# Turning the graph operator, the attention context and the gated input by DMA instead of on TensorE, in a four-layer graph kernel

## What is computed

```
x = LN(x + L0(x, adj))   # hypergraph convolution, relu, LN, convolution, + x
x = LN(x + L1(x, adj))   # softmax over nodes of q . (adj k), times v
x = LN(x + L2(x, adj))   # 8-head attention, scores times 2 adj
x = LN(x + L3(x, adj))   # gate from the row sums of adj, scores times adj

# L0's operator, used twice; H = (adj != 0)
P = Dn * (H @ (Be * H^T))         # Dn = 1 / (H w), Be = 1 / column counts
# L2
ctx = softmax(q k^T * scale * 2 adj) v ;  L2 = ctx Wo^T + bo
# L3
xg = x * sigmoid(deg * wd + bd) ;  QK = sigmoid(xg Wqk^T + bqk)
L3 = relu(normalised(QK QK^T * adj) xg Wl^T + bl + xg Wr^T)
```

## Time and profile before

| | |
|---|---|
| median of three runs | 952.0 us |
| the profiled execution | 954.0 us, span 952.2 us |
| PE, DVE, ACT, POOL busy, share of the span | 91%, 80%, 77%, 71% |
| mean granted PE clock | 0.974 |
| DMA packets, of these under 512 B | 194573, 112866 |

### The profile page before, as it was taken

The page is one execution under the profiler, slowest core; times in us unless marked ns, Lnnn a source line. Parts: engine busy times, 40 slices in busy tenths (PEclk is TensorE's granted clock), DMA queues, the critical chain, the costliest instruction groups (busy, mean ns, idle before and its releaser), DMA issues.

```text
span 952.2 us, 34347 instructions
## 1 busy us (share of the span) xinstructions
PE 871.1 (91%) x12124; PEld 755.5 (79%) x12124; DVE 764.7 (80%) x2292; ACT 730.8 (77%) x1740; POOL 678.1 (71%) x1005
## 2 busy tenths in 40 slices
PE   3668999999999999999999999999999999998754
PEld 2557778888888888888888888888888888886642
DVE  4757787888888888888888888888888888887651
ACT  2466578888888888888888888888888888877551
POOL 2566677778777778877877777887787777774440
PEclk9799899999999999999999999999999999999985
DMA  7003453443444344444444444444434443444420
GB/s 210 20 15 97 109 114 73 103 114 102 111 124 122 100 115 110 113 104 119 104 109 124 121 100 116 108 113 104 120 100 113 124 121 100 116 99 125 119 46 22
DMA packets 194573, 99.46 MB, mean 104 GB/s; under 512 B 112866, under 2 KB 194276, under 8 KB 194532
## 3 DMA queue, kind: packets, MB, share of 16 engines
q1 hardware_dynamic: 194532, 98.93, 40.5%
HBM read 48.28 MB, written 25.17 MB: 77 GB/s over the span
## 4 chain that ended last, share of the span: by engine, by line
PE 30%; SPq 22%; DVE 14%; DMA 14%; issue 10%; ACT 6%; POOL 3%; DVEq 0%; ACTq 0%; POOLq 0%
PE bank L537 7%; PE bank L538 7%; PE bank L539 7%; DMA Ks<-k_by_head 6%; SPq L426 6%; DMA k_by_head<-kst 6%; SPq L402 5%; SPq L374 3%; SPq L387 3%; DVE Ehl L1288 2%; DVE stG L1126 2%; PE bank L562 2%; PE bank L738 2%; DVE preG L1347 2%; PE bank L815 1%
## 5 line engine op out<-in xcount | busy, mean ns | idle before, releaser
L1375 POOL TENSOR_TENSOR rFl<-r,rFh 128x512 f16<-128x512 f32 x64 | 73.1, 1162 | 25.5 <-ACT rFh L826 25.5
L537 PE MATMUL bank<-z1h,W 128*128 128x256 f16 x256 | 71.7, 280 | 4.7 <-DVE z1l L1025 4.6
L538 PE MATMUL bank<-z1l,W 128*128 128x256 f16 x256 | 71.7, 280 | 0.0
L539 PE MATMUL bank<-z1h,W 128*128 128x256 f16 x256 | 71.6, 280 | 0.0
L1476 POOL TENSOR_TENSOR late<-late,Smx 128x512 f32<-128x512 f32 x64 | 66.1, 1051 | 5.5 <-DVE Smx L1282 5.5
L539 PE MATMUL bank<-W,rFl 128*128 128x256 f16 x256 | 69.8, 273 | 0.0
L538 PE MATMUL bank<-W,rFh 128*128 128x256 f16 x256 | 69.8, 273 | 0.0
L537 PE MATMUL bank<-W,rFh 128*128 128x256 f16 x256 | 69.8, 273 | 0.0
L857 ACT ACTIVATE late<-preG,nbG,rsG 128x256 f32<-128x256 f32 x64 | 34.9, 592 | 33.2 <-POOL nbG L1397 33.2
L1375 POOL TENSOR_TENSOR y0l<-y,y0h 128x512 f16<-128x512 f32 x32 | 37.1, 1161 | 26.2 <-ACT y0h L826 26.2
L886 ACT ACTIVATE r<-bank,b1c 128x256 f32<-128x256 f32 x128 | 49.8, 462 | 7.4 <-PE bank L539 7.4
(11 more groups left out here) (281 smaller groups left out, 4182.6 us busy)
## 6 DMA issues: line engine op xcount, KB each, us to landing
Qs<-q_by_head SPq DMA_DIRECT2D x96, 128.0 KB, 2.6
Ks<-k_by_head SPq DMA_DIRECT2D x96, 128.0 KB, 2.5
Vbd<-vst SPq DMA_DIRECT2D x128, 66.0 KB, 2.1
xin<-x SPq DMA_DIRECT2D x32, 256.0 KB, 2.9
q_by_head<-qst SPq DMA_DIRECT2D x32, 256.0 KB
k_by_head<-kst SPq DMA_DIRECT2D x32, 256.0 KB, 2.2
out<-late SPq DMA_DIRECT2D x32, 256.0 KB, 2.2
aC<-adj_mask SPq DMA_DIRECT2D x32, 65.0 KB, 2.2
```

The lines of the kernel that those rows point to most:

```text
L537: pe.matmul(o, sh, mh, start=start, stop=False, skip_group_check=True)
L538: pe.matmul(o, sh, ml, start=False, stop=False, skip_group_check=True)
L539: return pe.matmul(o, sl, mh, start=False, stop=stop, skip_group_check=True)
L1375: return pool.tensor_tensor(dst, a, b, ALU.subtract)
```

## The change

- P: ACT writes the scaled operator as f16 straight from PSUM into Ps, DVE subtracts its low part into Ps (two instructions, one per tile, that scale by Dinv again), and one DMA transpose of 128x512 (`turn_conv`) turns both parts of both tiles into Pt. PE's two turns and ACT's cast of Ph go.
- context: DVE divides in place in PSUM, ACT casts and DVE subtracts per tile into cxs, one DMA transpose of 128x1024 (`turn_cx`) makes cxT. PE's four turns go.
- gated input: DVE makes (tanh + 1) * x3 into PSUM in one instruction, ACT casts, DVE subtracts into xgs, one DMA transpose of 128x1024 (`turn_xg`) makes xgT. PE's four turns, ACT's g2 and POOL's product go.
- loads: the host lays adj out four ways, so that atA (with its zeros, which doubles its bytes), atG and the layer-1 mask come in one DMA per group each; the mask's two loads and the clear of atA go.
- all order tables are new.

```diff
-                pe.wait_ge(ev("p_f"), at.n())
-                for t in range(TILES):
-                    m = pe.transpose(bA[:, TOK + t * P:TOK + (t + 1) * P], Pf[:, t], ident[:])
-                m.then_inc(ev("p_turned0"), 1)
-                yield
-                pe.wait_ge(ev("p_lo"), at.n())
+                pe.wait_ge(ev("p_turned"), at.chain(16, 16))
...
+            def turn_conv(at):
+                sp.wait_ge(ev("p_lo"), at.n()).then_inc(ev("sp_held"), 1)
+                if at.earlier(2):
+                    sp.wait_ge(ev("conv2"), at.n(-2)).then_inc(ev("sp_held"), 1)
+                sp.dma_start_transpose(Pt[:, at.par].rearrange("p t l k -> p (t l) k"),
+                                       Ps[:].rearrange("p t l k -> p (t l k)")).then_inc(ev("p_turned"), 16)
...
+                for t in range(TILES):
+                    m = act.activation(Ps[:, t, 0], bA[:, t * P:(t + 1) * P], ACT.Copy, scale=Dinv[:, t:t + 1])
+                m.then_inc(ev("p_hi"), 1)
...
-                low(Pl[:, at.par].rearrange("p t k -> p (t k)"), bA[:, TOK:2 * TOK],
-                    Ph[:, at.par].rearrange("p t k -> p (t k)")).then_inc(ev("p_lo"), 1)
+                for t in range(TILES):
+                    m = low(Ps[:, t, 1], bA[:, t * P:(t + 1) * P], Ps[:, t, 0], Dinv[:, t:t + 1])
+                m.then_inc(ev("p_lo"), 1)
...
+                for t in range(TILES):
+                    dve.wait_ge(ev("cx_hi"), at.tile(t))
+                    hi, lo = [cxs[:, t, i].rearrange("p (h d) -> p h d", h=HEADS) for i in range(2)]
+                    dve.tensor_tensor(lo, weighted(t)[:, :, 0:HD], hi, ALU.subtract).then_inc(ev("cx_lo"), 1)
+                    yield
...
+                dve.scalar_tensor_tensor(out=bG[:].rearrange("p (t d) -> p t d", t=TILES), in0=gt[:], scalar=1.0,
+                                         in1=x3[:, at.par], op0=ALU.add, op1=ALU.mult).then_inc(ev("xg"), 1)
...
-                pool.tensor_tensor(xg[:], g2[:], x3[:, at.par], ALU.mult).then_inc(ev("xg"), 1)
...
-                for b in range(2):
-                    sp.dma_start(mrow[64 * b:64 * b + 64, at.par], mr[b, bass.ds(at.group(), 1)].broadcast_to(
-                        [64, TILES, NODES])).then_inc(ev(f"C_in{at.par}"), 16)
...
-                blocks(atA, adj_t, at, "at_in")
+                sp.dma_start(atA[:, at.par], at_group(adj_bd, at)).then_inc(ev(f"at_in{at.par}"), 16)
...
-ORDER_SP = [3, 3, 3, 5, 0, 0, 3, 3, 2, 0, 4, 2, 2]
+ORDER_SP = [3, 4, 0, 3, 4, 0, 0, 3, 5, 3, 3, 2, 4, 0, 2, 2]
```

More of the change, by code:

```diff
@@ L555, in project_tm, with project_turned, project_rows @@
                             k == 0 and not onto, k == chunks - 1 and not onto)
+                return m
+            def project_turned(o, W, aT):
+                for c in range(2):
+                    oc = o[:, c * TOK:(c + 1) * TOK].rearrange("p (t k) -> p t k", t=TILES)
+                    cols = slice(c * P, (c + 1) * P)
+                    for k in range(2):
+                        m = mm3(oc, W[:, 0, k, cols], W[:, 1, k, cols], aT[:, :, 0, k], aT[:, :, 1, k], k == 0, k == 1)
+                return m
+            def project_rows(o, aT, W, t, n=D, n0=0, onto=False):
+                for k in range(2):
+                    m = mm3(o, aT[:, t, 0, k], aT[:, t, 1, k], W[:, 0, k, n0:n0 + n], W[:, 1, k, n0:n0 + n],
+                            k == 0 and not onto, k == 1 and not onto)
                 return m
@@ L775, in stream5 @@
                 first_needs(at, 9)
-                pe.wait_ge(ev("xgF_lo"), at.n())
-                project_fm(bG, Wqk3, xgFh, xgFl).then_inc(ev("qk3"), 1)
+                pe.wait_ge(ev("xg_turned"), at.chain(16, 16))
+                project_turned(bG, Wqk3, xgT).then_inc(ev("qk3"), 1)
                 yield
@@ L976, in stream4 @@
                 yield
-                act.wait_ge(ev("cx_turned"), at.n())
-                cast(cFh[:].rearrange("p c k -> p (c k)"), bF0[:]).then_inc(ev("cF_hi"), 1)
-                yield
+                if at.earlier(1):
+                    act.wait_ge(ev("cx_turned"), at.chain(16, 16, -1))
+                for t in range(TILES):
+                    act.wait_ge(ev("cx"), at.tile(t))
+                    cast(cxs[:, t, 0].rearrange("p (h d) -> p h d", h=HEADS), weighted(t)[:, :, 0:HD]
+                         ).then_inc(ev("cx_hi"), 1)
+                    yield
                 if not at.earlier(1):
@@ L983, in stream4 @@
                 act.wait_ge(ev("gate_pre"), at.n())
+                if at.earlier(1):
+                    act.wait_ge(ev("xg"), at.n(-1))
                 act.activation(gt[:], gp[:], ACT.Tanh, scale=0.5).then_inc(ev("gate_tanh"), 1)
-                yield
-                act.wait_ge(ev("gate_tanh"), at.n())
-                act.activation(g2[:], gt[:], ACT.Copy, bias=1.0)
                 yield
@@ L992, in stream4 @@
                 yield
-                act.wait_ge(ev("xg_turned"), at.n())
-                cast(xgFh[:].rearrange("p c k -> p (c k)"), bG[:], 0.5 / WS).then_inc(ev("xgF_hi"), 1)
+                act.wait_ge(ev("xg"), at.n())
+                if at.earlier(1):
+                    act.wait_ge(ev("xg_turned"), at.chain(16, 16, -1))
+                cast(xgs[:, :, 0], bG[:].rearrange("p (t d) -> p t d", t=TILES), 0.5 / WS).then_inc(ev("xg_hi"), 1)
                 yield
@@ L1033, in low_biased @@
                 return m
-            dve.memset(atA[:], 0.0).then_inc(ev("const"), 1)
             dve.memset(onesf[:], 1.0).then_inc(ev("const"), 1)
```

168 lines of the change are left out of this document (84 added, 84 removed).

## The result

The changed kernel takes 974.96 us (median, 973.85 to 978.87) beside 952.15 us for the kernel before in the same session: a ratio of 1.025, 95% interval 1.0221 to 1.0279. It is slower by 2.5%, where 946 us was forecast, with a range up to 965. Its profiled execution has a span of 972.1 us, 19.9 more than before.

The account below looks back on a forecast made before the run. PE bound the kernel before; afterwards a round through DVE and PE of 25.8 us a step would. Loop -16, fill +5 and drain +5 gave -6 us: median 946 us, range 931 to 965, likeliest case alone 936 to 954.

Parts of the forecast that it names:

- The round that binds: Loop: a round from Dbg over DVE, PE and DVE to the next Dbg sets the step, 25.8 us against 26.47.
- PE's leg: Part of the round on PE, from the W1 product to the layer-3 output: 7.5 us.
- first leg: Part of the round on DVE, from Dbg to the end of z1l: 7.9 us.
- the four legs: Dbg to z1l 7.9 us, wait before W1 0, W1 to layer-3 residual 7.5, residual to next Dbg 10.4.
- the third leg: Round on DVE from layer-3 residual to next Dbg: 10.4 us, with the adjacency chain HT to HBh at 1.6.
- K behind Pt: SP's queue: K's fetch stands behind Pt; beside it the third piece lands 6.3 us after Dbg, PE needing it at 6.7.
- half that: SP's queue: Pt, with four blocks, was put at half the 1.4 us for which an eight-block transpose holds the queue.
- The rival of late scores: Loop: K's packets start only when Pt has landed, so scores come late; step 26.6, total 965 us; chance 0.22.
- Pt itself: Operator's DMA transpose: lands 2.9 us after issue, 5.2 after Dbg; PE needs it at 5.6, so hidden by 0.4.
- The fill: First steps: +7.5 us for Pt's landing, -2.5 for loads and set-up order, together +5, between 0 and +9.
- The drain: Last groups: twice +2 us for the gated input and about 1 for the context, +5, between +2 and +9.
- the gated leg: Drain, gated product to its first matmul: 3.4 us before, 5.4 with three wide operations and the DMA transpose.

Follow-up runs that it names:

- P on PE: Changed kernel with the operator P alone turned on PE in f32 again, no Pt transpose in the queue: 971.24 us, ratio 1.0211.
- the hold alone: Changed kernel with two loop reorderings, POOL's input bias behind y0l and DVE's statistics of preB ahead of Ql: 965.98 us, ratio 1.0152.
- the old tables: Changed kernel with the order tables of the kernel before in the first four steps: 975.17 us with Pt by DMA, 957.21 us with P on PE.
- The last version: Changed kernel with P on PE, the old tables, and POOL's input bias behind y0l and DVE's preB statistics ahead of Ql, loop only: 945.38 us, ratio 0.9951.

## Why the prediction was wrong, step by step

- **The round that binds** was right in its places: PE's turns went as counted, PE's leg took the 7.5 forecast, and DVE became the partner of the bound. That the steps with a short HBh take 25.7, where 25.8 was forecast, is in part luck: their first leg is 0.46 shorter than forecast, and a wait for K of 0.41, put at nothing, fills the place. On average the four legs differ from the forecast by -0.31, +0.49, 0 and +0.37: 0.55 a step or 13 us over 24 steps, which is what is missing between the 16 forecast and the 2.6 gained.
- **The step that failed in the loop** is the third leg, "HT to HBh, 1.6", with all of DVE's operations costed at their lengths in the earlier trace rows. In the kernel before, HBh was held in no step of the loop (251 ns on average over 48); after the reordering it was in every other. That puts (11.18 - 10.37) / 2 = 0.40 a step on the leg, 10 us over 24 steps. In the steps after a short leg DVE comes early and the first leg is 7.75 instead of 7.44, mostly waiting for ACT's high part of P. What the hold is worth by itself depends on the next wait: 0.31 a step with Pt in the queue (26.36 to 26.05), 0.46 without (26.17 to 25.71). The forecast asked what is queued behind a wait, never what runs beside an operation that is moved.
- **K behind Pt** failed too: "half that" for Pt's hold was wrong. Four blocks hold the queue for 1.20, nearly as long as eight, and the next issue comes 1.39 after Pt's, not 0.7. On average K's fetch goes out 3.9 after Dbg, with P on PE 2.9. So K's last piece lands some 7.3 after Dbg, just ahead of the scores, where 6.3 was computed, and the wait is about 0.5 a step. The short first leg hid it in the sum. Pt out of the queue gives back 0.19 a step (26.36 to 26.17), the hold alone 0.31, both together 0.65. The rival of late scores had the place right and the mechanism wrong: K still lands 2.5 after its issue, so its packets do not wait for Pt's; its issue does.
- **Pt itself** was right: landed 2.4 after its issue, against 2.9 assumed, and PE comes to it 5.1 after Dbg with nothing to wait for. So were the context and the gated input: PE waits for neither in the loop. The Trainium skill's price by block ("VectorE: DVE Perf Modes", The three transpose paths), by which Pt was estimated at 5.2, is not borne out.
- **The fill** is the second failed step: +5 assumed, 16.3 measured. The order of the set-up, which no row priced, was taken to give back 2.5; with P on PE the new tables cost 13.2. Dbg of group 0 came at 16.5 where it was at 11.7, since the set-up now goes first, and putting it behind, with Pt in place, was worse still (group 0 at 58.4). From Dbg to W1 groups 0 to 3 took 2.2, 1.5, 2.9 and 4.9 more than before, where +1.9 each was put for Pt's landing; but with the same tables and no Pt they take hardly less, so in the changed kernel most of this is the order. In the last, DVE has P's low part done only 3.3 after Dbg, behind a set-up piece, preB and v's low part; Pt lands at 6.1, and PE comes to it at 7.4. The 1.9 priced Pt's landing on an empty queue, and no row of it; under the old tables the runs show 17.2 for it. So either term alone was far off, and the two lie over each other. Which pieces of the new tables cost most stays open.
- **The drain** was right: +6.2 for +5, and the gated leg takes 5.3, summed as 5.4. The other runs with its drain tables lie from +5.3 to +9.4.

What stays open: the context's and the gated input's turns and the single loads were not undone by themselves. The last version shows that the three together with P on PE gain; which of them carries it was not tried.

## What to carry to other kernels

When an order changes, go through every DVE operation whose operands lie in SBUF and look at what POOL runs beside it in the new order; its length in the old trace holds only for its old neighbours. A transpose on a queue in fixed order is priced by its hold (here 1.2 us), not by its blocks, and whatever must follow it (here K) pays that first. The fill of a pipeline wants a price of its own: here the new order tables alone cost 13 us of it, and the new latency in the first stage alone 14 to 17.

## What was not expected of the hardware

A DMA transpose of four blocks holds SP's queue for 1.20 us and one of eight for 1.23 (cxT, at 474.78), so the hold hardly depends on the size; the landing does, 2.4 against 2.8 to 3.2. A shift of about 0.1 us between two engines decided between 0.42 and 1.46 us for the same pair, and the loop settled into an alternation of 25.7 and 27.0 that a mean of 26.4 hides. The same fill, run twice, gave the W1 products of group 1 in 2.52 us and in 4.80.
